# Layer one's gathers: one indirect gather in 32 is replaced by 128 single-row DMAs from SyncE and ScalarE

## The reference

```
def gcn_layer(x, W, b, w, src, dst):
    support = x @ W
    msgs = support[src] * w[:, None]
    return segment_sum(msgs, dst, num_segments=12500) + b
h = elu(gcn_layer(layernorm(x), W1, b1, edge_weight, src, dst))
h = elu(gcn_layer(h, W2, b2, edge_weight, src, dst))
x = x + h
x = x + routed_ffn(layernorm(x))
```

## Time and profile before

| | |
|---|---|
| median of 3 runs | 4681.69 us (4680.24 to 4682.98) |
| the profiled execution | span 4687.7 us, 6.0 us above the median |
| layer one's gathers | first at 89.9, last at 2056.4 us |
| layer two's gathers | first at 2075.8, last at 4075.2 us |
| busy share of the span | PE 74%, POOL 70%, DVE 42%, ACT 24% |

### The profile page before, as it was taken

How to read it: one execution, slowest core, us unless ns; L and a number is a source line. 1 busy time by engine, 2 the same in 40 slices (tenths; PEclk the granted TensorE clock), 3 DMA queues, 4 the chain that set the end, 5 groups by cost and what they waited for, 6 DMA issues and landing times.

```text
span 4687.7 us, 84720 instructions
## 1 busy us (share of the span) xinstructions
PE 3478.1 (74%) x21458; PEld 3215.9 (69%) x21459; DVE 1979.0 (42%) x6592; ACT 1116.6 (24%) x1692; POOL 3267.9 (70%) x3405
## 2 busy tenths in 40 slices
PE   2766676676666666667877777777777777859999
PEld 1666666665666665657777777777777777748887
DVE  8333333333333333334454454445444444573333
ACT  4111111111111111113333333333333333311111
POOL 5777777777777777767777777777777777524444
PEclk7766666667666666669999999999999999889999
DMA  8333333333333333334444444444444444335554
GB/s 278 113 113 112 113 111 112 113 112 112 113 111 113 112 113 112 113 95 128 145 139 144 144 137 143 145 144 139 141 145 139 142 143 145 116 127 169 180 175 150
DMA packets 266657, 627.24 MB, mean 134 GB/s; under 512 B 63397, under 2 KB 135034, under 8 KB 265922
## 3 DMA queue, kind: packets, MB, share of 16 engines
q0 software_dynamic: 170688, 492.87, 36.6%
q1 hardware_dynamic: 95362, 129.30, 7.9%
HBM read 519.25 MB, written 103.63 MB: 133 GB/s over the span
## 4 chain that ended last, share of the span: by engine, by line
PE 40%; issue 21%; POOL 15%; DVE 11%; DVEq 5%; DMA 5%; ACT 2%; POOLq 0%; ACTq 0%; SPq 0%
PE pA L1164 23%; POOL rows L537 15%; PE pA L1286 8%; PE pB L1202 4%; DMA rows<-xn_scratch,idx 3%; DVE S L847 2%; PE pZ L1174 1%; ACT L653 1%; DVE work L929 1%; DVEq L359 1%; PE pC L1276 1%; PE pB L1276 1%; DVE work L924 1%; DVEq L876 1%; DVE aggT L886 1%
## 5 line engine op out<-in xcount | busy, mean ns | idle before, releaser
L1164 PE MATMUL pA<-S,rows 128*128 128x96 f32 x12544 | 2040.8, 337 | 716.0 <-DVE S L847 314.5
L1164 PEld LDWEIGHTS pA<-S,rows 128*128 128x128 f32 x12544 | 1966.6, 249 | 834.3 <-issue 421.7
L537 POOL DMA_INDIRECT rows<-h_scratch,idx x1568 | 1502.3, 958 | 516.5 <-issue 492.5
L537 POOL DMA_INDIRECT rows<-xn_scratch,idx x1568 | 1490.2, 950 | 485.2 <-issue 458.1
L886 DVE TENSOR_TENSOR aggT<-aggT,pA 128x192 f32 x784 | 277.3, 354 | 2061.0 <-PE pA L1164 1421.4
L625 ACT ACT_TABLE_LOAD x196 | 251.5, 1283 | 3002.5 <-DVE aggT L886 3000.4
L847 DVE TENSOR_SCALAR S<-iota_w,tdst,twgt 128x96 f32<-128x96 f32 x3152 | 843.9, 343 | 5.5 <-issue 2.6
L1174 PE MATMUL pZ<-wg,stage 128*128 128x256 f32 x784 | 295.2, 514 | 252.6 <-ACT stage L625 252.6
L1202 PE MATMUL pB<-work,w 128*128 128x128 f32 x3232 | 389.2, 279 | 33.2 <-DVE work L929 33.2
L1202 PEld LDWEIGHTS pB<-work,w 128*128 128x128 f32 x3232 | 370.1, 192 | 42.0 <-DVE work L929 42.0
L1286 PE MATMUL pA<-aggT,work 128*128 x1680 | 381.7, 380 | 0.0
(11 more groups left out here) (175 smaller groups left out, 2107.9 us busy)
## 6 DMA issues: line engine op xcount, KB each, us to landing
pay_scratch<-work SPq DMA_DIRECT2D x98, 512.0 KB
rows<-xn_scratch,idx POOLq DMA_INDIRECT x1568, 2.8
rows<-h_scratch,idx POOLq DMA_INDIRECT x1568
h_scratch<-work SPq DMA_DIRECT2D x98, 128.0 KB
pay_scratch<-work SPq DMA_DIRECT2D x98, 128.0 KB, 2.5
work<-in_x_dram SPq DMA_DIRECT2D x97, 128.0 KB
rows<-in_x_dram SPq DMA_DIRECT2D x24, 512.0 KB, 5.2
xn_scratch<-rows SPq DMA_DIRECT2D x24, 512.0 KB, 5.9
```

What stands on the lines that cost most here:

```text
L537: pool.indirect_dma_start(rows[:, s, t, :], None, source, bass.IndirectOffsetOnAxis(at, 0))\
L1164: last = mm(to[:, k * W:(k + 1) * W], rows[:, slot, t, k * P:(k + 1) * P], Sx[:, t, :], start=(t == 0), stop=(t == T - 1))
```

## The change

In layer one the last of the 32 gathers of each iteration (slot 7, tile 3) is left out on POOL. Its 128 rows are fetched one by one: lanes 0 to 63 by SP, lanes 64 to 127 by ACT. Each of the two loads its 64 source indices of the next iteration into a one-row tile (xsrc), loads 32 of them at a time into registers, and issues 32 DMAs whose source address comes from a register. SP does its two batches of 32 back to back once the slot is free. ACT does one batch at the start of each half, ahead of that half's ticks. PE waits for SP's and ACT's rows before group 8i+7.

SP's loop of h1 stores is gone: ACT issues the store at the end of each tick, after waiting for DVE's elu, and DVE waits for the store of the tick before by s_h1st. The tables iota_w and tnum become slices of iota_p. Layer two keeps its 32 gathers.

```
+        def single_rows(eng, who, i, part, last):
+            lane0 = (0 if who == "sp" else XROWS) + part * XREGS
+            if part == 0:
+                hold(eng, s_mm[0], SLOTS * (i + 1))
+                hold(eng, s_xsrc[who], 16 * (i + 1))
+            _, values = nc.values_load_multi_w_load_instructions(
+                xsrc[who][0:1, part * XREGS:(part + 1) * XREGS], engines=[eng.engine], min_val=0, max_val=N - 1,
+                skip_runtime_bounds_check_because="a src is a node's number")
+            if (part + 1) * XREGS == XROWS and not last:
+                row_sources(eng, who, i + 1)
+            for n, v in enumerate(values):
+                eng.dma_start(rows[lane0 + n:lane0 + n + 1, SLOTS - 1, XT, :], xn_d[bass.ds(v, 1), :])\
+                   .then_inc(s_xrow[who], 16)
...
 SP:
-            sp.sem_inc(s_free[0], 1)
-            sp.wait_ge(s_elu[0], 2)
-            sp.sem_inc(s_free[0], 1)
-            with sp.Fori(0, NB) as b:
-                sp.wait_ge(s_elu[0], b + 3)
-                sp.dma_start(h1_d[block_of(b), :], hout).then_inc(s_h1st, 16)
-                sp.wait_ge(s_h1st, 16 * (b + 1))
-                sp.sem_inc(s_free[0], 1)
+            row_sources(sp, "sp", 0)
+            xn_stored(sp)
+            with sp.Fori(0, ITERS - 1) as i:
+                for part in range(XROWS // XREGS):
+                    single_rows(sp, "sp", i, part, False)
...
 POOL:
-                        for t in range(T):
+                        for t in range(XT if layer == 0 and s == SLOTS - 1 else T):
...
 ACT, in tick1:
+                act.wait_ge(s_elu[0], j + 2)
+                act.dma_start(h1_d[block_of(j - 1), :], hout).then_inc(s_h1st, 16)
...
+            def iteration1(i, last):
+                for half in range(2):
+                    single_rows(act, "act", i, half, last)
+                    h = 2 * i + half
+                    _, start, end = half_flags(act, h)
+                    ticks(act, start, end, lambda j: tick1(j, h))
...
 DVE, in elu:
-                    dve.wait_ge(s_free[0], j + 1)
+                    dve.wait_ge(s_h1st, 16 * (j + 1))
...
 PE, in edges_half:
+                    if layer == 0 and s == SLOTS - 1:
+                        pe.wait_ge(s_gath[layer][s], 16 * XT * (i + 1))
+                        pe.wait_ge(s_xrow["sp"], 16 * XROWS * (i + 1))
+                        pe.wait_ge(s_xrow["act"], 16 * XROWS * (i + 1))
```

More of the change, by code:

```diff
@@ L85, in bass_gnn_then_routed_ffn @@
     KWIN = (N - 1) // W
+    XT = T - 1
+    XROWS = P // 2
+    XREGS = 32
     LNC = NB // T
@@ L95, in bass_gnn_then_routed_ffn @@
     xn_d = nc.dram_tensor("xn_scratch", [N, C], f32, kind="Internal").ap()
-    h1_d = nc.dram_tensor("h1_scratch", [NPAD, C], f32, kind="Internal").ap()
+    h1_d = nc.dram_tensor("h1_scratch", [NPAD + P, C], f32, kind="Internal").ap()
     pay_d = nc.dram_tensor("pay_scratch", [NPAD, PAY], f32, kind="Internal").ap()
@@ L136, in bass_gnn_then_routed_ffn @@
         before = sb("before", [P, P])
-        iota_w = sb("iota_w", [P, W])
         stats = sb("stats", [P, LNB, T, 6])
@@ L161, in bass_gnn_then_routed_ffn @@
         prefer = sb("prefer", [P, NX])
-        tnum = sb("tnum", [P, NT])
         iota_p = sb("iota_p", [P, P])
+        iota_w, tnum = iota_p[:, 0:W], iota_p[:, 0:NT]
         node = sb("node", [P, NB])
@@ L167, in bass_gnn_then_routed_ffn @@
         etab = sb("etab", [1, NT], i32)
+        xsrc = {"sp": sb("xsrc_sp", [1, XROWS], i32), "act": sb("xsrc_act", [1, XROWS], i32)}
         flat = aggT[:, :, :].rearrange("p k n -> p (k n)")
@@ L229, in bass_gnn_then_routed_ffn @@
         s_const = sem("constants_ready")
-        NCONST = 12
+        NCONST = 10
         s_rows_clear = sem("edge_rows_padded")
@@ L254, in bass_gnn_then_routed_ffn @@
         s_gath = [[sem(f"rows_gathered_{l}_{i}") for i in range(SLOTS)] for l in range(2)]
+        s_xsrc = {e: sem(f"row_sources_loaded_{e}") for e in ("sp", "act")}
+        s_xrow = {e: sem(f"single_rows_loaded_{e}") for e in ("sp", "act")}
         s_S = [sem(f"S_ready_{l}") for l in range(2)]
@@ L372, in ticks, with xn_stored, row_sources @@
                                             "the table's last end is the number of blocks"))
+        def xn_stored(eng):
+            eng.wait_ge(s_xst[0], 16 * (LNI + 2))
+            for s in range(1, SLOTS):
+                eng.wait_ge(s_xst[s], 16 * LNI)
+        def row_sources(eng, who, i):
+            at = (NG - SLOTS - SLOTS * i) * GE + XT * P + (0 if who == "sp" else XROWS)
+            eng.dma_start(xsrc[who][:, :], src[bass.ds(at, XROWS)].rearrange("(a n) -> a n", a=1))\
+               .then_inc(s_xsrc[who], 16)
+        def single_rows(eng, who, i, part, last):
[11 more added lines that the diff above has]
+                   .then_inc(s_xrow[who], 16)
         @block.sync
@@ L429, in _ @@
                 sp.dma_start(b1col[:, :], ffn_b1.rearrange("(k p) -> p k", p=P)).then_inc(s_w, 16)
-            sp.sem_inc(s_free[0], 1)
-            sp.wait_ge(s_elu[0], 2)
-            sp.sem_inc(s_free[0], 1)
-            with sp.Fori(0, NB) as b:
-                sp.wait_ge(s_elu[0], b + 3)
-                sp.dma_start(h1_d[block_of(b), :], hout).then_inc(s_h1st, 16)
-                sp.wait_ge(s_h1st, 16 * (b + 1))
-                sp.sem_inc(s_free[0], 1)
+            row_sources(sp, "sp", 0)
[3 more added lines that the diff above has]
+                    single_rows(sp, "sp", i, part, False)
+            for part in range(XROWS // XREGS):
+                single_rows(sp, "sp", ITERS - 1, part, True)
             sp.sem_inc(s_free[1], 1)
@@ L505, in _ @@
                 pool.memset(t[:, :, NG:TBL], 0.0).then_inc(s_tbl_clear, 1)
-            for to, pattern, base, per_lane in ((iota_w, [[1, W]], 0, 0), (woff, [[W, KWIN + 1]], 0, 0),
+            for to, pattern, base, per_lane in ((woff, [[W, KWIN + 1]], 0, 0),
                                                 (prefer, [[-1, NX]], NX, 0), (iota_p, [[1, P]], 0, 0),
-                                                (tnum, [[1, NT]], 0, 0), (node, [[P, NB]], 0, 1)):
+                                                (node, [[P, NB]], 0, 1)):
                 pool.iota(to[:, :], pattern, base=base, channel_multiplier=per_lane,
@@ L523, in _ @@
                 if layer == 0:
-                    pool.wait_ge(s_xst[0], 16 * (LNI + 2))
-                    for s in range(1, SLOTS):
-                        pool.wait_ge(s_xst[s], 16 * LNI)
+                    xn_stored(pool)
                 else:
-                    pool.wait_ge(s_h1st, 16 * NB)
+                    pool.wait_ge(s_h1st, 16 * (NB + 2))
                 with pool.Fori(0, ITERS) as i:
@@ L667, in _ @@
                 act.sem_inc(sm, 1)
[L668 to L675, removed]
+            act.sem_inc(s_h1st, 16)
+            row_sources(act, "act", 0)
+            xn_stored(act)
+            def iteration1(i, last):
[4 more added lines that the diff above has]
+                    ticks(act, start, end, lambda j: tick1(j, h))
+            with act.Fori(0, ITERS - 1) as i:
+                iteration1(i, False)
+            iteration1(ITERS - 1, True)
+            tick1(NB, None)
+            with act.Fori(0, ITERS) as i:
+                for half in range(2):
+                    h = 2 * i + half
+                    _, start, end = half_flags(act, h)
+                    ticks(act, start, end, lambda j: tick2(j, h))
             for j in range(NB, NB + DEPTH):
@@ L962, in _ @@
                     for s in range(SLOTS):
-                        dve.wait_ge(s_gath[0][s], 16 * T * ITERS)
+                        dve.wait_ge(s_gath[0][s], 16 * (T if s < SLOTS - 1 else XT) * ITERS)
+                    for who in ("sp", "act"):
+                        dve.wait_ge(s_xrow[who], 16 * XROWS * ITERS)
                     for half in range(2):
@@ L1219, in edges_half @@
                     s, g = half * HALF + u, HALF * h + u
-                    pe.wait_ge(s_gath[layer][s], 16 * T * (i + 1))
+                    if layer == 0 and s == SLOTS - 1:
+                        pe.wait_ge(s_gath[layer][s], 16 * XT * (i + 1))
+                        pe.wait_ge(s_xrow["sp"], 16 * XROWS * (i + 1))
+                        pe.wait_ge(s_xrow["act"], 16 * XROWS * (i + 1))
+                    else:
+                        pe.wait_ge(s_gath[layer][s], 16 * T * (i + 1))
                     if with_overflow:
```

## The result

The changed kernel takes 5035.3 us (median of 4 runs, 5031.9 to 5040.8), the kernel before beside it 4682.3 us (4680.2 to 4687.8). The ratio is 1.0752, 95% interval 1.0737 to 1.0767. The forecast was 5058 us. The profiled execution spans 5039.0 us at a granted clock of 0.797 (before 0.806).

What follows compares the result with a forecast made beforehand. POOL's 1568 gather issues at 1.255 us were taken to bound layer one, 40.1 us an iteration. ACT's terms summed to 47.8 us, +376 us over 49 iterations, forecast 5058 us, range 4830 to 5450 us.

Steps and rivals of the forecast that it cites:

- rival A: Layer one: ACT's two batches between its ticks hold the last group; 47.8 us an iteration, 5058 us; chance 0.48 with E.
- T0: Layer one's iteration: the end of the last group's matmuls, from which the forecast counts its times; 1019.91 in the earlier trace.
- POOL's saving: POOL in layer one: 49 gathers of 1.255 us removed, 61.5 us of issue, forecast to disappear.
- SP fits: SP in layer one: its two batches take 29.6 us and are ready for the last group with 5 us left.
- The load of 32 values: Address load into registers before each batch: taken as 2 us, between bounds of 0.27 and 8.6 us.
- C: Address load: values loaded one by one, 8.6 us instead of 2.0, 5705 us as outer end; chance 0.20.
- POOL's waits: Promised sign in the trace: POOL's gathers no longer 0.30 us apart but with waits for PE's last group.
- a 3 us hole on ACT at the back edge: Promised sign in the trace: ACT stalls at its loop's jump as DVE does, for 3.2 us.
- Term 2: ACT's back edge in layer one: 0.1 + 3.2 us taken for the loop's jump; the other end was 0.1.
- B: ACT's back edge: no stall, tick of half 0 on time, 45.3 us an iteration, 4935 us; chance 0.22.
- D: ACT's rows: transfers hidden, POOL stays the bound, 61 us less, 4621 us; chance 0.07.
- E: SP and ACT slow each other, or single-row DMAs slow gathers; 0.49 us per row; chance within rival A's 0.48.

Runs made afterwards that it cites:

- experiment 1: Changed kernel with ACT's 64 rows left out, SP's rows, POOL's 31 gathers and ACT's store kept: 4623.6 us, ratio 0.9868.
- experiment 4: Changed kernel with all rows back on POOL's 32 gathers, keeping only ACT's store and the shared iota tile: 4688.0 us, ratio 1.0006.
- experiments 2 and 3: Changed kernel with 32 of ACT's 64 rows left out: first batch alone 4632.5 us, second batch alone 4847.8 us.
- experiments 5 to 12: Changed kernel with both ACT batches before half 0's tick (5, 12), a 64-lane POOL gather (6), or two row buffers (7 to 11): ratios 1.1041 to 1.2969.
- experiment 6: Changed kernel with one 64-lane gather on POOL in place of ACT's rows, SP fetching the other 64 lanes: ratio 1.1051.

## Why the prediction held, step by step

The forecast of 5058 us was 23 us (0.5%) above the measured median, and its mechanism, rival A, is in the main the one that the trace shows: ACT comes late to the tick of half 0, and the second batch stands behind it. The stall that was to make it late is not there. The eight terms against the iteration shown above:

| term | forecast us | measured us |
|---|---|---|
| 1. T0 to the end of the store's issue | 4.6 | 4.7 (to 1108.80) |
| 2. back edge | 3.3 | 0.8 (to 1109.60) |
| 3. first batch | 14.8 | 14.8 (to 1124.44) |
| 4. flags, then the tick of half 0 | 0.7 + 3.8 | 1.5 + 3.9 (to 1129.87) |
| 5. second batch | 14.9 | 15.7 (to 1145.55) |
| 6. landing, last group | 2.0 + 3.7 | 1.9 + 3.7 (to 1151.16) |
| sum | 47.8 | 47.1 |

**What was right.** POOL's saving (61.5 us; 60 in experiment 1) and that it disappears; the row at 0.40 us; that SP fits (31.3 us instead of 29.6, hidden in experiment 1, done 10 us before ACT); that the store costs nothing (experiment 4); that the late tick makes PE and DVE wait; and layer two unchanged. The load of 32 values, at 2.0 us (2.1), was luck: it had been a guess between 0.27 and 8.6, and it decided between A and C. Of the signs promised one is missing, and one came in another form: POOL's waits are there, but for DVE's index staging and not for the slots (it goes on at T0 + 2.6, 1 us after the indices are staged, and no wait of POOL's is put to PE).

**What was mis-sized.** The missing one is "a 3 us hole on ACT at the back edge". Term 2 measured 0.8 us for everything between the store's issue and the load: no stall of DVE's kind, though ACT has 256 instruction records in an iteration. This is 2.5 us too much in the forecast, 122 us over the layer. Two smaller terms ran the other way. The flags took 1.5 us instead of 0.7, 0.46 of it one load that took 0.27 before, and the second batch has a DMA of its own between load and rows, ACT's 0.47 us issue of the next 64 indices (L388), some 0.7 us with its register steps. It was named in the change and left out of the sum. Together 1.6 us, 78 over the layer. So errors cancelled, and the total is better than its parts, which is luck too: -2.5, +0.8, +0.8 and +0.2 in the rest. By the sum that is 0.7 us an iteration less than forecast, 34 us; 13 us come back behind layer one's last gather (32.3 us to the next layer's first instead of 19.4), which the forecast had no term for.

The stall was inferred from DVE's 3.20 us at its back edge; in the changed kernel DVE still stands some 3.0 us there, and not behind the tick of half 0. The Trainium skill (Runtime: NRT & Kernel Launch, Instruction fetch mechanics) says that a taken branch to a target outside the two blocks held forces a fetch before execution goes on. The Trainium skill (same page and section) gives a block as 256 instructions. So a turn of 256 records may well lie within two, and that it "would stall too" did not follow from this rule. The trace, with 0.8 us, agrees with a jump that stays inside; it doesn't show where the limit lies. The number of records is no measure of it either: DVE has 170 to 172 in a turn, fewer than ACT, but its code holds branches that are not taken and leave no record.

**The rivals.** B had the right premise, no stall at the back edge, and the wrong number: 45.3 us an iteration against 47.1. It took the tick to be due at T0 + 20.3 and ACT to be there in time. ACT came at T0 + 21.9, and DVE's adds were done at T0 + 16.6. A had taken the same T0 + 20.3. The difference lies in PE's third and fourth group of the half, which take 3.81 us where they took 7.35. The windows around them (stretch, then PE, PEld, DVE, ACT, POOL busy, PEclk, DMA share, GB/s), in the kernel before and in the changed one:

```profile
1032.60:1040.20 7.60, 7.35 (x32) 6.98 (x32) 2.74 (x11) 0.00 (x0) 5.77 (x7) 0.50 0.38 107
```
```profile
1116.20:1120.10 3.90, 3.81 (x32) 3.65 (x32) 2.58 (x10) 0.00 (x0) 2.98 (x4) 1.00 0.40 114
```

The granted clock is 0.50 (1.2 GHz) in the first and 1.00 (2.4 GHz) in the second. Ahead of it PE had stood 11.69 us for the rows of the last group, run that group at 0.50, and multiplied 32 times in 6.59 us. Counted over 48 iterations of each trace, the two groups take 5.1 us in the mean instead of 7.2, and the adds are done at T0 + 17.9 instead of T0 + 20.4. The prediction had taken the slower durations everywhere, because a PE that idles more gave the clock "no reason to rise"; that held for the last group (3.70 us at 0.50) and not here. A's sum didn't suffer, since the tick starts when ACT is there. But of the 5.3 us by which ACT was late without any stall, 3.7 come from the tick being due earlier and 1.6 from ACT.

C is excluded by the load's 2.1 us. The Trainium skill (Runtime: NRT & Kernel Launch, Instruction fetch mechanics) gives about 200 ns for each register for loads from HBM, which would make this load 6.4 us, an estimate. The trace doesn't agree for this load, which is from SBUF: 2.1 us is 66 ns a value.

D needed 0.21 to 0.30 us for a row and got 0.40: the three instructions stand one behind the other with 0.30 us, and the gaps between them make up the rest. E is excluded as a large effect: SP's issue is 0.225 us in the changed kernel, and POOL's gathers still take 946 ns.

**Why the cost isn't the sum of its parts.** The forecast's frame, a second batch that stands behind a tick, is shown by experiments 2 and 3. Alone, the first batch ends about when the tick is due (9 us), and the second runs from the tick on, and its rows are late for the last group (224 us). Together the first moves the tick, from T0 + 18.4 to T0 + 21.9 in the iterations shown, and with it the second, for 179 us more.

**What stays open.** The price of both batches ahead of the tick on a usual chip; whether two buffers with constant destinations reach 4623 us there; how the changed kernel fares on the chips of experiments 5 to 12, and what stretches the queues there; and why the clock is granted in full in one stretch and not in the other. No measured version beats the kernel before except those that leave rows out.

## What to carry to other kernels

Work that is threaded between the steps of an engine with its own deadlines costs what it delays, not what it takes: a batch of some 15 us cost 0.2 us an iteration at one place and 4.6 at the next. Before an engine is given DMAs, the time from its last step to the buffer's next use is to be compared with the load of the addresses and the issues; here that was 9.9 us for a load of 2.1 and 32 issues of 0.40. And every DMA issue between load and use belongs in the sum: the one left out here cost 0.5 us an iteration, 0.7 with its register steps.

## What the runs showed of the hardware that was not expected

- A load of 32 values from SBUF into registers takes 2.1 us on SP and ACT; one value takes 0.27.
- A DMA of one row of 1 KB with the source in a register is issued in 0.225 us on SP and 0.235 on ACT (medians), and the next starts 0.40 us after it. With the destination in a register too the issue takes 0.529 and 0.552 us, and a row is 32 packets instead of 2.
- An indirect gather of 64 lanes takes 902 to 907 ns, one of 128 lanes 949 in the median of the same run.
- ACT runs through a loop turn of 256 instruction records with 0.8 us for all of its back edge, where DVE, with some 170 records in a turn, stood 3.20 us.
- In the iteration of the changed kernel that is shown, the third and fourth group's 32 matmuls ran at a granted clock of 1.00 in 3.81 us, after PE had stood 11.69 us ahead of the last group; in the kernel before, where it had stood 1.24 us there, they had 0.50 and 7.35 us.
- On three other chips (experiments 5 to 12) the kernel before takes 1.41 to 1.48 times as long (6592 to 6920 us), and the unchanged layer two 3202.7 us instead of 2000.2 in experiment 6, while the median of SP's issue stays 0.225 us and the longest goes to 1.4.
